# Extra TensorE products in the idle stretches ahead of the turned rows of sequence 0

## The reference: what is computed

```python
x = x + _L0_xattn_ref(_layernorm(x, axis=-1), ctx_512, ...)
x = x + _L0_ffn_ref(_layernorm(x, axis=-1), ...)
x = x + _L1_xattn_ref(_layernorm(x, axis=-1), ctx_512, ctx_512, ...)
x = x + _L1_ffn_ref(_layernorm(x, axis=-1), ...)
```

```python
kv = k_v @ W_k.T + b_k
out = jnp.einsum('bij,bjd->bid', p, kv)
sim = jnp.einsum('bid,bjd->bij', out, kv) * scale
sim = (sim - mu) * jax.lax.rsqrt(var + EPS) * ln_gamma + ln_beta
attn = jax.nn.softmax(sim, axis=-1)
```

## Time and profile before

| | us |
|---|---|
| median of three runs | 1729.98 |
| the profiled execution | 1728.49 |
| its span, first to last instruction | 1726.6 |
| PE busy | 1642.8 |
| DVE busy | 1057.3 |
| ACT busy | 811.4 |
| POOL busy | 314.7 |

### The profile page before, as it was taken

One profiled execution on the slowest core, in us unless ns is written; L12 is line 12 of the kernel. 1 busy time (PEld: TensorE's weight loads), 2 busy tenths in 40 slices (PEclk: granted clock), 3 DMA queues, 4 the chain that ended last, 5 costly groups with the idle time before them and its releaser, 6 DMA issues. The chain is left out here.

```text
span 1726.6 us, 26857 instructions
## 1 busy us (share of the span) xinstructions
PE 1642.8 (95%) x9268; PEld 1323.0 (77%) x9268; DVE 1057.3 (61%) x2195; ACT 811.4 (47%) x1797; POOL 314.7 (18%) x359
## 2 busy tenths in 40 slices
PE   3799999899999999999999999999999999999998
PEld 2687887678998987877767777778777777688887
DVE  5787677765676637856776764577466554542222
ACT  4566554144766743435656664343455543421110
POOL 1233324351222206420011100453000000000000
PEclk9699999999999999999999999999999999999999
DMA  4235578698899977999899865889934444355661
GB/s 148 88 126 173 188 260 284 222 358 302 294 354 320 284 279 283 367 297 353 261 304 320 288 220 202 316 293 362 318 95 139 142 145 162 123 171 173 225 204 56
DMA packets 135589, 410.01 MB, mean 237 GB/s; under 512 B 16032, under 2 KB 30752, under 8 KB 131744
## 3 DMA queue, kind: packets, MB, share of 16 engines
q1 hardware_dynamic: 123552, 368.98, 62.1%
q0 software_dynamic: 11904, 39.33, 7.0%
HBM read 303.92 MB, written 104.33 MB: 236 GB/s over the span
## 5 line engine op out<-in xcount | busy, mean ns | idle before, releaser
L1359 PE MATMUL ps<-xT,gu 128*128 128x512 f32 (+1 forms) x1224 | 455.5, 372 | 21.1 <-DVE gu L1852 12.0
L1361 PE MATMUL ps<-xT,gu 128*128 128x512 f32 (+1 forms) x1224 | 441.1, 360 | 0.0
L1360 PE MATMUL ps<-xT,gu 128*128 128x512 f32 (+1 forms) x1224 | 440.6, 360 | 0.0
L1359 PEld LDWEIGHTS ps<-xT,gu 128*128 128x128 f32 x1224 | 233.4, 191 | 59.0 <-issue 25.0
L1361 PEld LDWEIGHTS ps<-xT,gu 128*128 128x128 f32 x1224 | 233.1, 190 | 35.3
L1360 PEld LDWEIGHTS ps<-xT,gu 128*128 128x128 f32 x1224 | 233.8, 191 | 29.2
L1359 PE MATMUL ps<-wd,hid 128*128 128x512 f32 x604 | 244.6, 405 | 10.2 <-issue 3.7
L1361 PE MATMUL ps<-wd,hid 128*128 128x512 f32 x604 | 237.3, 393 | 0.0
L1360 PE MATMUL ps<-wd,hid 128*128 128x512 f32 x604 | 237.3, 393 | 0.0
L1572 ACT ACTIVATE hid<-act 128x512 fp32r<-128x512 f32 (+1 forms) x174 | 99.8, 573 | 236.4 <-DVE act L1837 235.7
L1837 DVE TENSOR_TENSOR act<-act,ps 128x512 f32<-128x512 f32 (+1 forms) x174 | 106.6, 613 | 160.5 <-PE ps L1361 160.0
(11 more groups left out here) (267 smaller groups left out, 2697.1 us busy)
## 6 DMA issues: line engine op xcount, KB each, us to landing
gu<-w_dram SPq DMA_DIRECT2D x150, 512.0 KB, 5.6
raw<-in_ffn_w SPq DMA_DIRECT2D x65, 768.0 KB, 6.1
wd<-w_dram SPq DMA_DIRECT2D x96, 512.0 KB, 5.6
w_dram<-raw SPq DMA_DIRECT2D x48, 512.0 KB, 5.1
gu_third<-w_dram SPq DMA_DIRECT2D x42, 512.0 KB, 3.9
w_dram<-gu SPq DMA_DIRECT2D x16, 1024.0 KB, 9.5
raw<-in_ffn_w POOLq DMA_DIRECT2D x48, 256.0 KB, 5.0
QT<-q_dram SPq DMA_DIRECT2D x48, 256.0 KB, 6.9
```

The source lines that it names most:

```text
L1359: mm(out_ap, ah, bh, start=start, stop=False)
L1360: mm(out_ap, ah, bl, start=False, stop=False)
L1361: return mm(out_ap, al, bh, start=False, stop=stop)
```

## The change

A step `warm` is added to the list of sequence 0 in four places: after `kvturn`, after the second and after the fourth turned row tile of the first norm, and after the softmax numerators, ahead of the second norm. The first three issue 9, 4 and 4 MATMULs of 512 columns, of the key weights `wkh` with the context `cTh`; the fourth issues 48 transposes of the identity. All write PSUM bank 0, which nothing reads before `gate0` of tile 0 overwrites it. They wait for nothing and signal nothing, and PE alone takes part. The planner is given their costs (0.23 us a MATMUL, 0.15 us a transpose) and what they follow: `kvturn`, `rowt` of tile 1, `rowt` of tile 3 and `rn2`.

```diff
-        ticks = [[("cload", b)]] * (b > 0) + [[("ctx", b)]] + pieces("stats1", b, 2 + ROOT) + [[("kv", b)], [("kvturn", b)]]
+        ticks = [[("cload", b)]] * (b > 0) + [[("ctx", b)]] + pieces("stats1", b, 2 + ROOT) + [[("kv", b)], [("kvturn", b)]] + [[("warm", 0)]] * (b == 0)
         for i in range(TB):
             ticks += [[("rown", 0, b, i)], [("rowt", 0, b, i)]]
+            if b == 0 and i % 2:
+                ticks.append([("warm", 1 + i // 2)])
...
-        ticks += [[("bet", b, i)] for i in range(TB)] + [[("aexp", b, i) for i in range(TB)]]
+        ticks += [[("bet", b, i)] for i in range(TB)] + [[("aexp", b, i) for i in range(TB)]] + [[("warm", 3)]] * (b == 0)
...
+    WARM = (9, 4, 4, 48)
...
+            "warm": [("PE", (0.15 if b_ == 3 else 0.23) * WARM[b_ % 4])],
...
+            "warm": lambda: [("kvturn", 0)] if b == 0 else [("rn2",)] if b == 3 else [("rowt", 0, 0, 2 * b - 1)],
...
+                elif kind == "warm":
+                    for _ in range(WARM[a[0]]):
+                        if a[0] == 3:
+                            turn(ps[:, 0, 0:P], ident[:, :], ident[:, :])
+                            continue
+                        mm(ps[:, 0, :], wkh[:, :], cTh[:, :], start=True, stop=True)
```

More of the change, by code:

```diff
@@ L313, in steps @@
             "bet": [("DVE", 0.75)], "aexp": [("ACT", 0.72)], "resid": [("DVE", 0.85)], "xh": [("POOL", 1.25)], "logit": [("PE", 0.95), ("DVE", 0.1)],
-            "xm": [("POOL", 1.0) if b_ else ("DVE", 0.65)], "xt": [("ACT", 0.53), ("DVE", 0.6)], "top2": [("DVE", 1.4)], "weights": [("ACT", 0.33), ("DVE", 1.2)], "ranks": [("PE", 0.36), ("DVE", 0.4)],
+            "warm": [("PE", (0.15 if b_ == 3 else 0.23) * WARM[b_ % 4])], "xm": [("POOL", 1.0) if b_ else ("DVE", 0.65)], "xt": [("ACT", 0.53), ("DVE", 0.6)], "top2": [("DVE", 1.4)], "weights": [("ACT", 0.33), ("DVE", 1.2)], "ranks": [("PE", 0.36), ("DVE", 0.4)],
             "before": [("DVE", 1.1)], "blocks": [("DVE", 1.2)], "places": [("DVE", (0.7, 1.9, 2.5)[min(b, 2)])], "slots": [("DVE", (1.9, 1.3)[min(b, 1)])], "hot": [("DVE", 0.65)], "spot": [("PE", 0.42)], "rowno": [("DVE", 0.15)], "xs": [("POOL", 2.55)],
```

## The result

The changed kernel takes 1715.9 us, the median of six runs (1713.37 to 1721.09), against 1729.08 us for the kernel before in the same comparison: a ratio of 0.9922 (95% interval 0.9901 to 0.9943), 13.2 us or 0.8% faster. The profiled execution is the slowest of the six, 1721.09 us, so its trace shows 7.4 us of the gain (1728.49 us in the profiled execution before).

What follows compares the result with a forecast made beforehand. PE, busy nearly throughout, was taken as the bound, so only its idle or slow time could be won: 1728.49 less 3.2 for the first norm gives 1725.3 us, a median forecast of 1726.8 us, range 1717.5 to 1732.5.

Steps and rivals of the forecast that it cites:

- The first norm: First norm: MATMULs hidden, clock high from 13.6 us; turned rows 1.4 us and `pkv` 1.8 us sooner, 3.2 us in sum.
- The rival by which the clock falls back between the rows: First norm: clock lost between turned rows, `pkv` as slow as before but 1.4 us earlier at most; 1728.6 us, chance 0.15.
- The 48 transposes: After `rn2`, ahead of the second norm's rows: hidden, 0.9 us to spare at the low clock; gain taken as nothing.
- The row that I leaned on: Second norm from 50.30 us: PE busy without idle pause on transposes and products of 8 columns, clock still 0.50.
- The rival's first half: Second norm: the 48 transposes raise the clock; the whole rival claimed 4 us more, 1722.8 us, chance 0.27.
- The step that failed: From the feed-forward's start, put at 65.3 us, to the end: the rest of the span as long as before.
- costs in the opening move all side streams alike, and the main stream with them: Planned order behind the opening: argument against a worse plan, a case priced at 5.9 us, chance 0.10.
- the gain is handed on whole: Behind the first norm: a pure chain up to 50.30 us with PE waiting passes on the full 3.2 us.
- The rival that came true: First experts' weights: by luck of the plan PE's 8.39 us wait for DVE vanishes; 1718.4 us, chance 0.10.
- My own tell for this case: First feed-forward product to the end: a distance differing by more than 2 us means the plan, not the clock.
- The two rivals on the plan: First experts' weights: plan worse by one group, 1732.7 us, or better without the wait, 1718.4 us; chance 0.10 each.
- the case of a plan that stays neutral: Whole kernel: time the same within 0.5%, between 1721.3 and 1738.6 us, chance 0.80.

Runs made afterwards that it cites:

- old_order_all: Kernel before with its order on every engine kept and all 65 new instructions put into PE's order: 1726.47 us, ratio 0.9973.
- old_order_first_norm: Kernel before with its order kept and only the 17 MATMULs of the first norm put in, no transposes: 1727.11 us, ratio 0.9977.
- plan_of_transposes_only: Changed kernel with the planner told only the cost of the 48 transposes and no new instruction issued: 1738.35 us, ratio 1.0060 to the kernel before.
- plan_only: Changed kernel with its orders as they are and none of the new instructions issued: 1721.47 us, ratio 0.9938 to the kernel before.

## Why the prediction was wrong

**The first norm** was right in its size: by its own steps 3.2 us, in the trace 3.07, alone in the old order 3.3. The nine MATMULs are hidden, and in the profiled execution the clock is high from the first turned rows on. The rival by which the clock falls back between the rows is half true: it does so in five of eight traces and costs 0.5 to 0.8 us, but the price of that rival was a slow `pkv`, and `pkv` is at the high clock in all eight.

**The 48 transposes** were right in time (taken as 0, measured between +1.2 and -0.6 us in the old order, the second being old_order_all less old_order_first_norm) and wrong in the reason. I said "transposes 0.2 us apart to the end of the 48", as plain busyness with such work had not raised the clock after 50.30 us. They were 0.109 us apart once the clock had risen. The row that I leaned on is an unbroken run too (before, PE pauses for no more than 0.04 us from 50.30 to 65.04 us at a clock of 0.50), but it has router products of 8 columns among the transposes, and with 80 transposes the clock fell behind just such products. So it was not "made of the same work", and the router products are the likely difference; no run separates them. The rival's first half happened (the clock is high before the 48 are through), its second did not: the faster transposes end 5.40 us ahead of the rows, and the clock is gone by then. "It needs the clock to outlast the last wait" was the condition, and it failed. With 80 it held, for 1.6 us of the 4 that I had priced. By the Trainium skill (TensorE: Matmul & The Clock Gate, section PE-mode transpose) the full clock does not engage for transposes; here the measurement differs: from 38 us to 42.42 they ran 0.109 us apart at a granted clock of 1.00 with no other product on PE. Whether they could raise it alone no run shows, since the eight products of `rn2` stood directly ahead each time.

**The step that failed** is "the rest of the span as long as before", that is, the new order entered in the sum as 0 and left to two rivals of 0.10 each. The measured effect of the order alone is -8.9 us, more than twice that of the instructions (-3.9). The argument against it, that "costs in the opening move all side streams alike, and the main stream with them", is false for this planner: the new step stands on PE and in sequence 0's stream alone, and nine MATMULs of cost were enough to change the orders hundreds of steps on. A small part goes the other way: "the gain is handed on whole" holds to the second norm's rows (3.05 us less from the first statistics on), but the new order gives 1.1 us of it back ahead of the feed-forward.

**The rival that came true** had its place and its wait right (the routing steps ahead of the weight split, the 8.39 us gone) and its size wrong: 8.39 us for the wait but nothing for what the wait does to PE. In the changed kernel's trace the waits and the low clock behind them make 11.3 us less between 280 and 345 us; moving the two steps alone gave 5.2. The trace of before held the clock's part already: 0.43 us steps behind 317.93 us. My own tell for this case was a distance from the first feed-forward product to the end that differs by more than 2 us: it differs by 5.9 (-7.3 less -1.4).

**The chances.** The two rivals on the plan were given 0.20 together and at most one group of steps each. The runs show orders from 8.3 us slower to 12.3 us faster for three sets of costs. That one of them came out better was no merit of the change: its own reason, the clock, is worth the smaller part, and the rest is luck in the planner's search. With a spread like that the case of a plan that stays neutral, which I had given 0.80 in all, was the least founded number of the forecast.

**Left open:** some 4 us of the order's gain that the moved routing steps do not give; why both profiled executions of the changed kernel lose some 4 us behind n = 1140; whether that is why they lie 5.2 and 3.6 us over the medians of their runs, since only those two were profiled; what in the planned order makes plan_of_transposes_only late at n = 540; and the 48 transposes in the new order.

## What to carry to other kernels

Where a program orders its own instructions, a filler step has two effects, its instructions and what its cost does to the order, and each has to be measured alone; a forecast should give the order the spread that other small changes of cost have shown, not zero. In this kernel small DVE operations ahead of something that PE needs were cheap where POOL had no wide ones (1.9 us for the seven) and dear beside them (5.90 and 8.19 us). Filler that is to keep PE's clock high has to last nearly until its consumer arrives: 48 transposes ended 5.40 us too soon and gave the second norm nothing, 80 ended 1.70 us ahead of it and gave it 1.6 us.

## What the runs showed of the hardware

A SCALAR_TENSOR_TENSOR of 128 by 23 on DVE takes 0.244 us ahead of POOL's wide products (median in plan_only), and 0.962 us in the kernel before and 1.190 us in plan_of_transposes_only beside POOL's TENSOR_TENSOR of 128 by 512. POOL in order of time, kernel before:

```profile
305.38 5.46 POOL L1312 TENSOR_TENSOR k_mul<-k_mul,k_rot 128x512 f32<-128x512 f32 x4
...
310.92 4.03 POOL L1318 TENSOR_TENSOR k_mul<-k_mul,krs 128x512 f32<-128x512 f32 x4
```

and the seven operations, as a group, kernel before:

```profile
L2034 DVE SCALAR_TENSOR_TENSOR r_tile_f<-r_block_no,r_first,r_tile_f x7: 243/962/1233, 309.6 to 315.3; 128x23 f32<-128x23 f32 x7
```

The first of the seven runs beside the last of the first group. The next four run beside the second group, whose operations follow each other 4.03 / 4 = 1.01 us apart, and the median of the seven is 0.962 us; the last two come behind them and take 0.24 us each. In the changed kernel six of the seven run beside POOL's operations of 128 by 128 (the group, then POOL in order of time):

```profile
L2045 DVE SCALAR_TENSOR_TENSOR r_tile_f<-r_block_no,r_first,r_tile_f x7: 380/385/1328, 278.6 to 281.1; 128x23 f32<-128x23 f32 x7
...
278.05 0.46 POOL L1211 TENSOR_TENSOR ksin<-kwB,sinB 128x128 f32<-128x128 f32 x1
278.47 0.46 POOL L1211 TENSOR_TENSOR kcos<-kwB,cosB 128x128 f32<-128x128 f32 x1
```

Those follow each other 0.42 us apart, and the median is 0.385 us. The small operations' time goes with the length of POOL's: it looks as if each of DVE's waited for one of POOL's. The Trainium skill (SBUF — State Buffer, section SBUF: two separate sides) has it that an operation of DVE with two inputs from SBUF and one of GpSimd take a shared port for the whole instruction, and the other waits; the durations agree. I had the 0.84 us each in front of me and took them as their price rather than as three parts waiting to one part work.

Transposes alone kept the granted clock at 1.00 from 38 us to their end at 42.42, and with 80 of them until 47.49 us. And before its first change in a trace the clock's column can be 1.00 while the clock is low: in the kernel before it is 1.00 from 20 to 24 us, where MATMULs are 0.43 us apart. In that stretch the distance between starts tells the clock and the column does not.
